# A transformer block in compensated float32: new order of the on-chip memories, MLP weight loads at the value steps, and the first values projected in two steps

## The chip, the cores and the metric

The kernel runs on one core of one Trainium2 chip. Its time is device microseconds (us) of that core, the median of several executions. Before the change it is 1606.38 us, the median of 3 executions (1605.19 to 1607.81).

## What is computed

The input is 16 sequences of 256 tokens with 256 features, 4096 tokens in all. Everything is float32.

```python
x = L0_attn_x                                   # (16, 256, 256)
x = x + layernorm(attn(layernorm(x)))           # 16 heads of 128, causal softmax, W_Q/K/V/O with biases
x = x + layernorm(ffn(layernorm(x)))            # MLP of 2048, gelu(gate) * up, then down
# attn: q, k, v = x @ W_Q, W_K, W_V + biases; scores = q k^T / sqrt(128); softmax; z = attn v; out = z W_O + b_O
# ffn weights: 4-bit codes from a table of 16 values, times one scale for each block of 32
```

## The kernel before

**Arithmetic.** Each float32 operand of a matmul is kept as a rounded high part and a remainder, in two memories whose names end in hi and lo. A product is three matmuls: hi times hi, hi times lo, lo times hi (the helper `three`, L691 to L694). ScalarE (ACT) writes the high part of a fresh PSUM result, VectorE (DVE) the low part by subtraction; for the probabilities and the weights GpSimd (POOL) makes the low part.

**Attention.** The tokens are worked in 8 chunks of 512 (2 sequences). A chunk has 16 steps, one for each head, so there are 128 steps, and n is the step's number, c = n // 16 its chunk and j = n % 16 its place in the chunk. `step_plan(n)` (L97) lists what a step holds, and all engines follow the list in order, each doing its own part. In step n TensorE projects queries and keys of head n+1 (`q`, `k`: 12 matmuls of 512 columns), adds head n-3 to the output projection (`out`), makes `z` of head n-2 and the scores of head n+1. `T` is the turning of the probabilities of head n: VectorE transposes 32x32 blocks of them into `turned`, SyncE's queue (SP) sends that to HBM (`send`, 384 KB) and fetches it back in four pieces (`fetch`, into `back`), which completes the transpose. `pT` is the copy of `back` into high and low parts for `z`. Once in four steps (n % 4 == 1) the values of four heads are projected, four token tiles with 6 matmuls each (`("v", t)`); tiles 0 and 2 are split into high and low parts (`v_hi`, `v_lo`), tiles 1 and 3 are copied whole (`v_late`) for float32 matmuls. The step n = 0 holds the values of the first four heads, all four tiles.

**PSUM.** Three banks (`fbank`) take turns for q, k, v, z and the turned input. A matmul group may start in a bank only when the result three places earlier was read: `bank_free` (L696) waits for VectorE's low part, or for ScalarE's copy of a `v_late` tile.

**Weights of attention.** They are loaded in pairs (256 KB) into `w_raw`, which has room for two pairs. ScalarE copies a pair into its high part (`weights_hi`, L611), GpSimd subtracts to get the low part (`weights_lo`, L1204), and only then may SyncE load the pair after next (L441). Two pairs a step are handled from step 0 on. The projection of head m's queries waits for its pair's low part (L758).

**SyncE.** One queue issues all DMAs in program order: in each step `send`, the pair loads, `fetch`, then whatever else the step has. `fetch` waits until `send` has landed.

**MLP weights.** In chunks 1 to 6 the engines expand the 4-bit MLP weights piece by piece and store them to HBM. After the last use of an attention weight in the last chunk (c = 7), its place in SBUF is filled with MLP weights: 24 units of two loads of 256 KB (`load_w4`, L426). Three units belong to two MLP columns of 128, of which there are 16; TensorE waits for all three before the first gate product of the two (L724). The MLP then runs over 8 chunks, from SBUF alone.

```python
        if c == NCH - 1 and j >= 2:
            load_w4(j - 2)
    for unit in range(HEADS - 2, PIECES // 2):
        load_w4(unit)
```

In chunks 1 to 7 SyncE also stores the block of x after attention of the chunk before in two halves, in steps j = 11 and 13 (`store_x1`). VectorE may write the next chunk's normalised input into the same memory (`stream`, L908) only after both have landed (L937).

Of the kernel before, what the change touches and what calls it, by code (L numbers as in the profile page):

```python
# [4 lines left out]
F32 = mybir.dt.float32  # L5
# [6 lines left out]
P = 128  # L12
# [84 lines left out]
def step_plan(n):  # L97
# [12 lines left out]
    if n == 0:  # L110
        return [("q", 1), ("k", 1), ("scores", 0), *values, ("T", 0), ("scores", 1)]
# [10 lines left out]
    return plan + values if n > 1 and n % HG == 1 else plan  # L122
# [78 lines left out]
class Memory:  # L201

    def __init__(self, nc, ctx):
        def sb(name, shape, dt=F32):
# [4 lines left out]
        self.mask = sb("mask", [P, SEQ])  # L209


        big = sb("weights", [P, 2, PIECES * 2 * P], F32R)
        qk_size = HEADS * 2 * KT * E
        self.wqk_p = [big[:, s, 0:qk_size].rearrange("p (h m k e) -> p h m k e", m=2, k=KT, e=E)
                      for s in range(2)]
        self.wv_p = [big[:, s, qk_size:].rearrange("p (h k e) -> p h k e", k=KT, e=E)
                     for s in range(2)]
        self.w4_all = [big[:, s, :].rearrange("p (n r e) -> p n r e", r=2, e=P) for s in range(2)]
        self.wo_p = [sb(f"wo_{s}", [P, HEADS, D], F32R) for s in ("hi", "lo")]
        self.raw = sb("w_raw", [P, RAW, 2, D])  # L220
# [6 lines left out]
        self.x_res = sb("x_res", [P, TT, D])  # L227
        self.stream = sb("stream", [P, TT, D])
        self.xnT = [sb(f"xnT_{s}", [P, KT, CHUNK], F32R) for s in ("hi", "lo")]
# [49 lines left out]
        self.hbank = [self.ubank[(2 * STEPS_ALL - UB + i) % UB] for i in range(3)]  # L279

# [135 lines left out]
def load_program(sp, mem, s, x_v, w_pairs, biases, words_v, scales_v, w4_v, x1_v, turned_v, out_v):  # L416
# [9 lines left out]
    def load_w4(unit):  # L426
# [8 lines left out]
        for part in range(2):  # L435
            sp.dma_start(mem.w4_all[part][:, at:at + 2].bitcast(F32),
                         w4_v[part][:, 2 * unit:2 * unit + 2]).then_inc(s.w4_all[q], 16)
# [70 lines left out]
    for n in range(STEPS_ALL):  # L508
# [22 lines left out]
        if c == NCH - 1 and j >= 2:  # L531
            load_w4(j - 2)
    for unit in range(HEADS - 2, PIECES // 2):
        load_w4(unit)
# [9 lines left out]
    for c in range(NCH):  # L544
        if c == NCH - 2:
            sp.wait_ge(s.y_stored, 16)
        if c < NCH - 1:

            if c:
                sp.wait_ge(s.xT, c * KT)  # L550
            else:
                sp.wait_ge(s.xn, NCH)
            sp.dma_start(mem.x_in[:], chunk(x1_v, c + 1)).then_inc(s.x, 16)
        if c == NCH - 1:
# [134 lines left out]
def tensor_program(nc, pe, mem, s):  # L689
# [31 lines left out]
    def gate_up(n):  # L721
# [3 lines left out]
        for up, banks in ((0, mem.gbank), (1, mem.hbank)):  # L725
            for kt in range(KT):
                piece = w4_place(3 * (i // 2) + i % 2) + up
                last = three(banks[slot(n)][:], [p[:, piece, kt, :] for p in mem.w4_all],
# [93 lines left out]
    for c, j, kind, m in MLP_STEPS:  # L822
# [16 lines left out]
        else:  # L839
# [6 lines left out]
            for t in range(TT):  # L846
# [3 lines left out]
                             [p[:, k:k + 2, m % 2, :] for p in mem.w4_all],  # L850
# [487 lines left out]
```

## Time and profile before

| | before |
|---|---|
| median of 3 executions | 1606.38 us (1605.19 to 1607.81) |
| profiled execution, its own time | 1606.72 us |
| its span in the trace | 1604.8 us |
| TensorE busy | 1577.9 us, 98% of the span |
| VectorE / ScalarE / GpSimd busy | 66% / 61% / 44% |
| mean granted TensorE clock | 0.998 |

The span is what the trace covers; the own time adds the launch around it (1.9 us). TensorE's busy share says how little it stands still in all (27 us), and its waits by releaser say where. The granted clock is the share of full speed that TensorE had in a stretch: 1.00 is 2.4 GHz, 0.5 is 1.2 GHz.

### The profile page before, as it was taken

The page shows a single profiled execution, that of the slowest core. Times are in us where ns is not written, and L with a number is a line of the kernel's source. Part 1 is how long each engine was busy: PE and PEld are TensorE (multiplying, and loading weights), DVE is VectorE, ACT ScalarE, POOL GpSimd, SP SyncE. Part 2 cuts the span into 40 slices and gives each one's busy share as a digit, 9 for nine tenths or more (in the row PEclk, how much of TensorE's full clock was granted, in tenths as well). Part 3 has the DMA queues.
Part 4 walks back from the last instruction along what each step waited for, and adds up shares of the span by engine and source line. Part 5 has one row for each costly group of instructions (what it writes and reads, how often), then busy time and mean ns, then how long its engine had stood idle before and what let it go on. Part 6 is the DMA issues. An engine that isn't in the chain of part 4 may idle for free.

```text
span 1604.8 us, 28430 instructions
## 1 busy us (share of the span) xinstructions
PE 1577.9 (98%) x9600; PEld 1398.1 (87%) x9600; DVE 1060.9 (66%) x3074; ACT 975.6 (61%) x2433; POOL 711.6 (44%) x1069
## 2 busy tenths in 40 slices
PE   6999999999999999999999999999999999999998
PEld 5888899889888988888889888888888888888887
DVE  4666677677767677677767766665656556565665
ACT  5887677767776777677767766644444444444443
POOL 5764455445554455455445533333333333333333
PEclk9999999999999999999999999999999999999999
DMA  4653434434443444443444455561000010000000
GB/s 122 186 172 116 129 128 149 142 116 142 149 139 119 142 142 137 127 151 126 142 128 136 142 157 162 155 214 40 27 14 27 14 40 27 14 28 14 27 15 25
DMA packets 157440, 167.69 MB, mean 104 GB/s; under 512 B 15856, under 2 KB 130672, under 8 KB 157296
## 3 DMA queue, kind: packets, MB, share of 16 engines
q1 hardware_dynamic: 157296, 165.89, 32.8%
q8 instruction: 76, 1.25, 0.3%
q14 instruction: 68, 0.56, 0.1%
HBM read 94.53 MB, written 71.30 MB: 103 GB/s over the span
## 4 chain that ended last, share of the span: by engine, by line
PE 85%; DMA 6%; ACT 3%; DVE 2%; SPq 2%; issue 1%; POOL 1%; DVEq 0%; POOLq 0%
PE fbank L692 14%; PE fbank L694 14%; PE fbank L693 14%; PE obank L694 7%; PE obank L693 7%; PE obank L692 7%; PE ubank L692 5%; PE ubank L693 5%; PE ubank L694 5%; PE ubank L716 3%; DMA turned_scratch<-turned 3%; PE fbank L794 3%; DMA back<-turned_scratch 2%; SPq L494 2%; ACT probs L589 1%
## 5 line engine op out<-in xcount | busy, mean ns | idle before, releaser
L692 PE MATMUL fbank<-xnT_hi,weights 128*128 128x512 f32 x768 | 305.8, 398 | 1.1 <-DVE xnT_lo L870 1.1
L693 PE MATMUL fbank<-xnT_lo,weights 128*128 128x512 f32 x768 | 304.7, 397 | 0.0
L694 PE MATMUL fbank<-xnT_hi,weights 128*128 128x512 f32 x768 | 304.6, 397 | 0.0
L1238 POOL TENSOR_TENSOR pT_lo<-back,pT_hi 128x512 fp32r<-128x512 f32 x128 | 165.9, 1296 | 284.9 <-ACT pT_hi L654 284.9
L600 ACT ACTIVATE w_raw<-fbank 128x512 f32<-128x512 f32 x128 | 76.4, 597 | 262.7 <-PE fbank L694 262.7
L1200 POOL TENSOR_SCALAR probs<-probs,rsum 128x128 f32<-128x128 f32 (+1 forms) x512 | 208.9, 427 | 20.6 <-DVE rsum L893 16.7
L694 PEld LDWEIGHTS fbank<-xnT_hi,weights 128*128 128x128 f32 x768 | 145.1, 189 | 35.2
L885 DVE CUSTOM_DVE_ANT_0 probs<-ubank,mask 128x128 f32<-128x128 f32 (+1 forms) x512 | 155.0, 355 | 29.1 <-PE ubank L694 28.3
L692 PEld LDWEIGHTS fbank<-xnT_hi,weights 128*128 128x128 f32 x768 | 145.2, 189 | 27.0 <-DVE xnT_lo L870 1.5
L693 PEld LDWEIGHTS fbank<-xnT_lo,weights 128*128 128x128 f32 x768 | 145.2, 189 | 24.7
L974 DVE SCALAR_TENSOR_TENSOR w_raw<-w_raw,fbank 128x512 f32<-128x512 f32 x128 | 87.9, 687 | 113.3 <-ACT w_raw L600 113.3
L1218 POOL TENSOR_TENSOR kT_lo<-probs,kT_hi 128x512 fp32r<-128x512 f32 x64 | 82.8, 1293 | 165.6 <-ACT kT_hi L609 165.6
L980 DVE SCALAR_TENSOR_TENSOR probs<-w_raw,fbank 128x512 f32<-128x512 f32 x128 | 88.0, 687 | 97.9 <-ACT w_raw L604 97.9
L570 ACT ACTIVATE zT_hi<-fbank,bias_v 128x512 fp32r<-128x512 f32 x128 | 87.5, 684 | 106.6 <-PE fbank L794 106.3
L1218 POOL TENSOR_TENSOR v_lo<-probs,v_hi 128x512 fp32r<-128x512 f32 x64 | 82.7, 1292 | 156.4 <-ACT v_hi L609 156.4
L692 PE MATMUL obank<-wo_hi,zT_hi 128*128 128x256 f32 x512 | 143.6, 280 | 0.0
L694 PE MATMUL obank<-wo_hi,zT_lo 128*128 128x256 f32 x512 | 143.4, 280 | 0.0
L693 PE MATMUL obank<-wo_lo,zT_hi 128*128 128x256 f32 x512 | 142.8, 279 | 0.0
L872 DVE SCALAR_TENSOR_TENSOR kT_lo<-fbank,bias_k,kT_hi 128x512 fp32r<-128x512 f32 x128 | 95.8, 749 | 58.9 <-ACT k_early L581 58.6
L1043 DVE STREAM_TRANSPOSE turned<-probs 128x384 f32<-128x384 f32 x256 | 131.5, 552 | 0.7 <-DMA turned_scratch<-turned 0.7
L589 ACT ACTIVATE probs<-probs,nmax 128x256 f32<-128x256 f32 x256 | 126.7, 495 | 0.0
L587 ACT ACTIVATE probs<-probs,nmax 128x128 f32<-128x128 f32 x256 | 100.7, 394 | 15.3 <-DVE nmax L885 11.6
(122 smaller groups left out, 4571.9 us busy)
## 6 DMA issues: line engine op xcount, KB each, us to landing
turned_scratch<-turned SPq DMA_DIRECT2D x128, 384.0 KB, 2.6
back<-turned_scratch SPq DMA_DIRECT2D x512, 96.0 KB, 2.2
w_raw<-in_w_pairs SPq DMA_DIRECT2D x32, 256.0 KB, 3.3
w_hi_scratch<-w_hi SPq DMA_DIRECT2D x48, 128.0 KB, 2.0
w_lo_scratch<-w SPq DMA_DIRECT2D x48, 128.0 KB, 2.0
weights<-w_hi_scratch SPq DMA_DIRECT2D x24, 256.0 KB, 3.6
weights<-w_lo_scratch SPq DMA_DIRECT2D x24, 256.0 KB, 4.1
x_res<-in_x SPq DMA_DIRECT2D x16, 256.0 KB, 2.9
```

The lines of the kernel that those rows point to most:

```text
L587: act.activation(pr[:, 0:P], pr[:, 0:P], ACT.Exp, bias=nmax[:, 0:1], scale=-1.0, accum_out=sums[:, 0:1])
L589: act.activation(pr[:, P:384], pr[:, P:384], ACT.Exp, bias=nmax[:, 1:2], scale=-1.0, accum_out=sums[:, 1:2]).then_inc(s.exp, 1)
L692: nc.tensor.matmul(out, a[0], b[0], start=start, stop=False, skip_group_check=skip)
L693: nc.tensor.matmul(out, a[0], b[1], start=False, stop=False, skip_group_check=skip)
L694: return nc.tensor.matmul(out, a[1], b[0], start=False, stop=stop, skip_group_check=skip)
L872: ins = dve.scalar_tensor_tensor(dst, bank, bias, hi.bitcast(F32), ALU.add, ALU.subtract)
L885: last = dve.tensor_tensor_reduce(out=pr[:, lo:hi], in0=bank[:, lo:hi], in1=mask, scale=-SCALE, scalar=3.0e38, op0=ALU.add, op1=ALU.min, a ...
L980: after(dve.scalar_tensor_tensor(act_v, mem.th[j % 2], 1.0, mem.gbank[slot(n)][:], ALU.add, ALU.mult))
L1043: dve.transpose(mem.turned[:, :, :, b, :].rearrange("p k u j -> p u k j"), mem.probs[b].rearrange("p (u k j) -> p u k j", u=3, k=4)).then_ ...
L1200: last = pool.tensor_scalar(pr[:, lo:hi], pr[:, lo:hi], mem.rsum[i][:, at:at + 1], 1.0, ALU.mult, ALU.mult)
L1218: pool.tensor_tensor(lo, mem.act_v[j % 2], hi.bitcast(F32), ALU.subtract).then_inc(s.iT_lo, 1)
L1238: pool.tensor_tensor(lo[:].rearrange("p u b (a j) -> p (u b) a j", j=32), mem.back[m % 2][:, :, 0:2].rearrange("p a u b j -> p (u b) a j") ...
```

## The change

It has three parts.

1. The order of the SBUF memories. `stream`, `x_res` and `xnT` move from behind the weights to the front, `mask` moves behind the weights, and the one memory `weights`, which held the query/key and the value weights of both parts, becomes four (`wqk_hi`, `wqk_lo`, `wv_hi`, `wv_lo`). A helper `w4_at` finds an MLP piece in them. Sizes and operands are the same.
2. In the last chunk SyncE loads MLP weights only in the steps in which values are projected (j = 1, 5, 9, 13), two units each; 6 more follow behind the last attention step, and the last 10 behind the first load of x of the MLP stage.
3. The first values are projected in two steps: tiles 0 and 1 in step 0, tiles 2 and 3 in step 1, behind the projections of head 2.

```diff
@@ step_plan
     if n == 0:
-        return [("q", 1), ("k", 1), ("scores", 0), *values, ("T", 0), ("scores", 1)]
+        return [("q", 1), ("k", 1), ("scores", 0), *values[:2], ("T", 0), ("scores", 1)]
+    if n == 1:
+        return [("q", 2), ("k", 2), *values[2:], ("T", 1), ("pT", 0), ("scores", 2)]
@@
-    return plan + values if n > 1 and n % HG == 1 else plan
+    return plan + values if n % HG == 1 else plan
@@ Memory
-        self.mask = sb("mask", [P, SEQ])
+        self.stream = sb("stream", [P, TT, D])
+        self.x_res = sb("x_res", [P, TT, D])
+        self.xnT = [sb(f"xnT_{s}", [P, KT, CHUNK], F32R) for s in ("hi", "lo")]
-        big = sb("weights", [P, 2, PIECES * 2 * P], F32R)
...
+        self.wqk_p = [sb(f"wqk_{s}", [P, HEADS, 2, KT, E], F32R) for s in ("hi", "lo")]
+        self.wv_p = [sb(f"wv_{s}", [P, HEADS, KT, E], F32R) for s in ("hi", "lo")]
         self.wo_p = [sb(f"wo_{s}", [P, HEADS, D], F32R) for s in ("hi", "lo")]
+        self.mask = sb("mask", [P, SEQ])
@@
+    def w4_at(self, part, piece):
+        if piece < 2 * HEADS:
+            return self.wqk_p[part][:].rearrange("p h m k e -> p (h m) k e")[:, piece:]
+        return self.wv_p[part][:, piece - 2 * HEADS:]
@@ load_program, in a step
-        if c == NCH - 1 and j >= 2:
-            load_w4(j - 2)
-    for unit in range(HEADS - 2, PIECES // 2):
+        if c == NCH - 1 and j % HG == 1:
+            for unit in (j // 2, j // 2 + 1):
+                load_w4(unit)
+    for unit in range(HEADS // 2, HEADS - 2):
         load_w4(unit)
@@ load_program, MLP
             sp.dma_start(mem.x_in[:], chunk(x1_v, c + 1)).then_inc(s.x, 16)
+        if c == 0:
+            for unit in range(HEADS - 2, PIECES // 2):
+                load_w4(unit)
```

Where SyncE's instructions stand shows part 2. Before, in steps j = 11 and 12 of the last chunk (`back` is the fetch, `x_scratch` the store of x, `weights` the MLP loads):

```order
L484 DMA turned_scratch<-turned 128x768
L494 DMA back<-turned_scratch 32x4x192 x4
L458 DMA x_scratch<-stream 128x2x256
L436 DMA weights<-w_hi_scratch 128x512
L436 DMA weights<-w_lo_scratch 128x512
L484 DMA turned_scratch<-turned 128x768
L494 DMA back<-turned_scratch 32x4x192 x4
L436 DMA weights<-w_hi_scratch 128x512
L436 DMA weights<-w_lo_scratch 128x512
L484 DMA turned_scratch<-turned 128x768
```

The same steps of the changed kernel, and step 13 behind them, up to its first MLP loads:

```order
L488 DMA turned_scratch<-turned 128x768
L498 DMA back<-turned_scratch 32x4x192 x4
L462 DMA x_scratch<-stream 128x2x256
L488 DMA turned_scratch<-turned 128x768
L498 DMA back<-turned_scratch 32x4x192 x4
L488 DMA turned_scratch<-turned 128x768
L498 DMA back<-turned_scratch 32x4x192 x4
L462 DMA x_scratch<-stream 128x2x256
L440 DMA wqk_hi<-w_hi_scratch 128x512
L440 DMA wqk_lo<-w_lo_scratch 128x512
```

Between the send of step 11 and that of step 12 there were two MLP loads, and between those of steps 12 and 13 two more; both pairs are gone.

ScalarE's instructions of step 1 show part 3. Before, from the projections of head 2 to the copy of the probabilities of head 0:

```order
L570 ACTIVATE qT_hi<-fbank,bias_q 128x256
L575 ACTIVATE q_early<-fbank,bias_q 128x256
L570 ACTIVATE kT_hi<-fbank,bias_k 128x512
L581 ACTIVATE k_early<-fbank,bias_k 128x256
L613 ACTIVATE wo_hi<-w_raw 128x512
L613 ACTIVATE weights<-w_raw 128x512
L654 ACTIVATE pT_hi<-back 128x512
```

In the changed kernel:

```order
L578 ACTIVATE qT_hi<-fbank,bias_q 128x256
L583 ACTIVATE q_early<-fbank,bias_q 128x256
L578 ACTIVATE kT_hi<-fbank,bias_k 128x512
L589 ACTIVATE k_early<-fbank,bias_k 128x256
L621 ACTIVATE wo_hi<-w_raw 128x512
L621 ACTIVATE wqk_hi<-w_raw 128x512
L577 ACTIVATE v_hi<-fbank 128x512
L577 ACTIVATE v_late<-fbank 128x512
L662 ACTIVATE pT_hi<-back 128x512
```

The copies of value tiles 2 and 3 now stand behind the two weight copies (`wo_hi` and `wqk_hi`) and ahead of `pT_hi`. On VectorE the low part of tile 2 stands before the transpose of head 1 where nothing stood between that and the low part of the keys. Before:

```order
L872 SCALAR_TENSOR_TENSOR qT_lo<-fbank,bias_q,qT_hi 128x256
L872 SCALAR_TENSOR_TENSOR kT_lo<-fbank,bias_k,kT_hi 128x512
L1043 STREAM_TRANSPOSE turned<-probs 128x3x4x32 x2
L885 ISA probs,nmax<-ubank,mask 128x128
L885 ISA nmax 128x1
```

After:

```order
L880 SCALAR_TENSOR_TENSOR qT_lo<-fbank,bias_q,qT_hi 128x256
L880 SCALAR_TENSOR_TENSOR kT_lo<-fbank,bias_k,kT_hi 128x512
L878 TENSOR_TENSOR v_lo<-fbank,v_hi 128x512
L1051 STREAM_TRANSPOSE turned<-probs 128x3x4x32 x2
L893 ISA probs,nmax<-ubank,mask 128x128
```

So the transpose and the masking of head 2's scores (the ISA rows) come behind `v_lo`, which needs ScalarE's `v_hi`.

## Rows read from the trace of the kernel before

**Rows 1.** The page: busy time of each engine

```profile
PE 1577.9 (98%) x9600; PEld 1398.1 (87%) x9600; DVE 1060.9 (66%) x3074; ACT 975.6 (61%) x2433; POOL 711.6 (44%) x1069
```

**Rows 2.** Waits of TensorE: us in total, times, longest us

```profile
PE fbank L692 <- DVE v_lo L870: 5.5, 5, 3.5
PE ubank L716 <- DVE kT_lo L872: 3.8, 6, 1.9
...
PE fbank L711 <- DVE stream L908: 0.9, 2, 0.6
```

**Rows 3.** Windows of the last chunk: length, busy times, clock, DMA share, GB/s

```profile
1027.50:1031.20 3.70, 0.24 (x2) 0.04 (x1) 1.02 (x3) 3.68 (x12) 2.88 (x5) 1.00 0.61 221
1031.20:1035.60 4.40, 4.40 (x12) 3.49 (x13) 1.49 (x4) 0.74 (x2) 0.01 (x1) 0.61 0.78 208
```

**Rows 4.** Timeline, steps 12 and 13 of the last chunk: start us, us

```profile
1015.44 0.43 SPq L458 DMA_DIRECT2D x_scratch<-stream  x1
1015.97 0.41 SPq L436 DMA_DIRECT2D weights<-w_hi_scratch  x1
...
1016.98 0.38 SPq L484 DMA_DIRECT2D turned_scratch<-turned  x1
1022.78 2.93 SPq L494 DMA_DIRECT2D back<-turned_scratch  x4
...
1027.52 0.63 ACT L654 ACTIVATE pT_hi<-back 128x512 fp32r<-128x512 f32 x1 [4.45 <-DMA back<-turned_scratch]
...
1031.16 0.50 PE L692 MATMUL fbank<-weights,xnT_hi 128*128 128x512 f32 x1 [3.46 <-DVE v_lo L870]
```

**Rows 5.** Timeline of SyncE, step 12 of the chunk before

```profile
887.61 0.41 SPq L484 DMA_DIRECT2D turned_scratch<-turned  x1
890.53 1.74 SPq L494 DMA_DIRECT2D back<-turned_scratch  x4
```

**Rows 6.** Timeline, second store of x, last chunk

```profile
1032.42 0.43 SPq L458 DMA_DIRECT2D x_scratch<-stream  x1
...
1034.80 1.38 DVE L908 TENSOR_SCALAR stream<-x_in,mv,rstd 128x256 f32<-128x256 f32 x4 [2.73 <-DMA x_scratch<-stream]
```

**Rows 7.** Timeline of steps 0 and 1

```profile
19.32 0.40 PE L692 MATMUL fbank<-weights,xnT_hi 128*128 128x512 f32 x1
...
24.62 2.53 POOL L1207 TENSOR_TENSOR weights<-w_raw,weights 128x512 fp32r<-128x512 f32 x2
...
25.01 0.69 DVE L870 TENSOR_TENSOR v_lo<-fbank,v_hi 128x512 fp32r<-128x512 f32 x1 [0.27 <-ACT v_hi L569]
...
27.05 0.95 SPq L442 DMA_DIRECT2D w_raw<-in_w_pairs  x2
...
32.20 1.03 DVE L1043 STREAM_TRANSPOSE turned<-probs 128x384 f32<-128x384 f32 x2
32.34 0.49 PE L716 MATMUL ubank<-k_early,q_early 128*128 128x128 f32 x2 [1.93 <-DVE kT_lo L872]
...
32.65 0.63 ACT L613 ACTIVATE wo_hi<-w_raw 128x512 fp32r<-128x512 f32 x1 [1.15 <-DMA w_raw<-in_w_pairs]
...
34.37 0.63 ACT L654 ACTIVATE pT_hi<-back 128x512 fp32r<-128x512 f32 x1 [0.40 <-DMA back<-turned_scratch]
```

**Rows 8.** DMA issues: form, count, KB each, median us from issue to landing

```profile
w_raw<-in_w_pairs SPq DMA_DIRECT2D x32, 256.0 KB, 3.3
...
weights<-w_hi_scratch SPq DMA_DIRECT2D x24, 256.0 KB, 3.6
```

**Rows 9.** Timeline of TensorE, first and ninth matmul of MLP column 4

```profile
1062.01 0.40 PE L692 MATMUL fbank<-xnT_hi,weights 128*128 128x512 f32 x1
...
1063.88 0.39 PE L694 MATMUL ubank<-xnT_hi,weights 128*128 128x512 f32 x1
```

**Rows 10.** Groups of TensorE with 256 columns: count, busy us, mean ns, idle

```profile
L693 PE MATMUL obank<-wo_lo,zT_hi 128*128 128x256 f32 x512 | 142.8, 279 | 0.0
...
L693 PE MATMUL ubank<-kT_lo,qT_hi 128*128 128x256 f32 x256 | 71.9, 281 | 0.0
```

More of the change, by code:

```diff
@@ L208, in __init__ @@
         self.power = sb("power", [P, TT])
-        self.mask = sb("mask", [P, SEQ])
-        big = sb("weights", [P, 2, PIECES * 2 * P], F32R)
[L213 to L219, printed above, removed]
+        self.stream = sb("stream", [P, TT, D])
[3 more added lines that the diff above has]
+        self.wv_p = [sb(f"wv_{s}", [P, HEADS, KT, E], F32R) for s in ("hi", "lo")]
+        self.wo_p = [sb(f"wo_{s}", [P, HEADS, D], F32R) for s in ("hi", "lo")]
+        self.mask = sb("mask", [P, SEQ])
         self.raw = sb("w_raw", [P, RAW, 2, D])
@@ L226, in __init__ @@
         self.x_in = sb("x_in", [P, TT, D])
-        self.x_res = sb("x_res", [P, TT, D])
-        self.stream = sb("stream", [P, TT, D])
-        self.xnT = [sb(f"xnT_{s}", [P, KT, CHUNK], F32R) for s in ("hi", "lo")]
         self.qT = [[sb(f"qT{i}_{s}", [P, 2, P], F32R) for s in ("hi", "lo")] for i in range(2)]
@@ L435, in load_w4 @@
         for part in range(2):
-            sp.dma_start(mem.w4_all[part][:, at:at + 2].bitcast(F32),
+            sp.dma_start(mem.w4_at(part, at)[:, 0:2].bitcast(F32),
                          w4_v[part][:, 2 * unit:2 * unit + 2]).then_inc(s.w4_all[q], 16)
@@ L727, in gate_up @@
                 piece = w4_place(3 * (i // 2) + i % 2) + up
-                last = three(banks[slot(n)][:], [p[:, piece, kt, :] for p in mem.w4_all],
+                last = three(banks[slot(n)][:], [mem.w4_at(p, piece)[:, 0, kt, :] for p in range(2)],
                              [p[:, kt, :] for p in mem.xnT], kt == 0, kt == KT - 1)
@@ L849, in tensor_program @@
                 last = three(out, [p[:, t * P:(t + 1) * P] for p in mem.iT[m % 4]],
-                             [p[:, k:k + 2, m % 2, :] for p in mem.w4_all],
+                             [mem.w4_at(p, k)[:, 0:2, m % 2, :] for p in range(2)],
                              m == 0 and t % 2 == 0, m == NT - 1, skip=True)
```

## The prediction

> **What bounds the kernel now.** I read the page first. TensorE is busy 1577.9 of 1604.8 us and no other engine over 1061 [rows 1], so only its 27 us of standing still, and stretches in which it runs slowly, can be won. The change adds and removes no matmul. The waits of TensorE by releaser come next. The two large entries that the edits can touch are the wait for `v_lo`, 5.5 us in five waits of which one is 3.5, and the wait for `kT_lo`, 3.8 us in six of which one is 1.9 [rows 2]. The timeline places them: the 3.5 is at 1031.16, in step 13 of the last chunk, ahead of value tile 3 [rows 4]; the 1.9 is at 32.34, ahead of the scores of head 2, in step 1 [rows 7]. Windows around the first show what comes with it: TensorE does nothing from about 1027.5 to 1031.2, and in the 4.40 us behind that its granted clock is 0.61 on the mean, most of it the lower level of 1.2 GHz [rows 3].
>
> **MLP loads at the value steps.** Follow the wait at 1031.16 back. TensorE waits for a PSUM bank that VectorE's `v_lo` frees; that waits for `v_hi` on ScalarE, which works in order, behind `pT_hi` and the exponentials; and `pT_hi` began at 1027.52, after 4.45 us of idleness, on the landing of `back` [rows 4]. The fetch for it was issued at 1022.78, the moment the send of 1016.98 had landed, 5.8 us after its issue. Ahead of that send in the queue are the store of x (1015.44) and one unit of MLP loads, the first at 1015.97 [rows 4]. One chunk earlier the same send has the same store ahead (it stands in the same step) and no such unit, and lands after 890.53 - 887.61 = 2.9 us [rows 5]. So 2.9 us of the lateness belong to the unit that the change removes here. The next unit, between fetch and next send, goes too.
>
> What remains of the wait? `pT_hi` would start 2.9 us earlier, at about 1024.6. The exponentials, `v_hi` and `v_lo` behind it took from 1027.52 to 1031.16; shifted they end at 1028.3, against a need at 1027.7 (1031.16 - 3.46). That leaves 0.6 us. But the issue of the fetch took 2.93 us there against 1.74 one chunk earlier [rows 4, 5], at a place in time that the shifted fetch would have passed by then, which is worth 1.2 us more; so I take 0 as left, with 0.6 as the other end. Without a long wait the slow stretch goes too: 4.40 us at 0.61 lose 4.40 x 0.39 = 1.7 us [rows 3]. Gain: 3.46 + 1.7 = 5.2 us.
>
> Where the stall goes: TensorE now asks for the next chunk's normalised input 5.2 us earlier. VectorE writes it only when the second half of x is stored; before, the store was issued at 1032.42 and VectorE began at 1034.80 [rows 6]. The store stands behind the fetch of step 13, whose send gets 3 to 4 us earlier (it no longer waits for the late fetch and the unit), not 5.2, so it becomes the next to be late. In the other chunks this very wait occurs twice, 0.9 us in all, 0.6 at most [rows 2]. I take 0.4 us, with 0 and 1.5 as ends. In the new value steps four loads (1 MB) go out behind the fetch; a value step is longest before the next send, and one load lands in 3.6 us [rows 8], so these I cost at nothing. If that cover failed, a send would be late as at 1016.98, again some 3 us.
>
> The ends of the loads: 6 units are issued behind the last attention step instead of 10, and the last 10 behind one load of x. MLP column 4 starts at 1062.01 [rows 9] and needs units 6 to 8; unit 8 is now the first of the burst, issued where unit 14 is now, about 10 us ahead of that, and needs 3.6 us [rows 8]. Each later pair of columns has more slack than it loses. I cost this at nothing.
>
> **First values in two steps.** TensorE has the same work ahead of the scores of head 2 in either order: tiles 2 and 3 only change places with the scores of head 1 and the projections of head 2. In the new order the queries of head 2 come at about 23.3 (the values begin at 19.32 [rows 7], two tiles take 12 x 0.234 = 2.8 us by [rows 9], the eight shorter matmuls of head 1's scores some 1.2) and wait for the low part of their weights, the first of the two GpSimd instructions that begin at 24.62 and take 2.53, so until 25.9 [rows 7]. Behind it stand 24 matmuls; the ninth starts 1.87 us behind the first [rows 9], so 0.234 each, 5.6 us, and the scores of head 2 come at 31.5 instead of 32.34: 0.8 us earlier [rows 7], the wait of 1.93 filled by matmuls.
>
> Against this stands what now lies in the way of head 1's transpose. It must wait for `v_lo` of tile 2, that for `v_hi`, and that for two weight copies; the first of these starts at 32.65, when a load issued at 27.05 has landed, 5.6 us later [rows 7]. The median of such a load is 3.3 us [rows 8]. In step 0 the transpose of head 0 loses a `v_lo` ahead of it (0.69 us at 25.01), so the send and the load behind it leave about 0.8 us earlier. Case A, the load is as slow as before: first copy at 31.8, second done at 33.1, `v_hi` and `v_lo` 1.3 us behind, so the transpose begins at 34.3 instead of 32.20 [rows 7], and the steps behind it, which in this phase are a chain from masking to exponentials to the next queries, come 1.2 to 1.8 us later. TensorE stood still 1.9 us at 32.34, has no slack to absorb it, and the whole kernel ends that much later. Case B, the load takes its median: it lands at 29.5, the copies end by 31.4, the transpose begins at 32.7, 0.5 late, while ScalarE, which before was held by `pT_hi` until 35.00 [rows 7] and now gets `back` earlier with the send of head 0, starts its exponentials about as early as before: -0.4 to 0.3 us. The landing is what decides, and both kinds stand in the trace; I take B, as only one load of the first steps was that slow, and 0.0 us. The gain is nothing: the filled wait of 1.93 is given back, because what bounds these steps is the chain, not TensorE.
>
> **Memory order.** Same sizes, same access patterns. The rows that could show a dependence on place are the 256-column matmuls: moving `wo` from one end of SBUF takes 279 ns, moving `kT` from the other 281 [rows 10]. I cost it at nothing. The 512-column matmuls follow each other every 0.234 us [rows 9]. The Trainium skill, TensorE: Matmul & The Clock Gate, gives 215.7 ns start to start for a warm back-to-back matmul of 512 columns, measured on other operands. If the present placement were what costs the difference, and the new one cured it, some 3840 matmuls would save 18 ns each, an estimate from that page of 70 us; by the rows here it saves 0, and the sum goes by the rows.
>
> **Sum.** -5.2 + 0.4 + 0.0 = -4.8 us against the profiled execution's 1606.72, whose own time stands 0.34 above the median. Median after: 1606.38 - 4.8 = 1601.6 us.
>
> **Rivals.**
> - Case A in step 1: the late weight load holds up `v_hi`. For it: 5.6 us for that load [rows 7]. Against: the median of 3.3 [rows 8]. Sum -4.8 + 1.5 = -3.3: 1603.1 us.
> - The clock falls in the first steps. The wait for the weights of head 2 is 25.9 - 23.3 = 2.6 us, between 1.93, after which TensorE kept its clock [rows 7], and 3.46, after which it fell [rows 4, 3]. If it falls, the 12 projections of head 2 take twice as long, 2.8 us more, straight on the chain; with the late copies some 3.5 us in all. Sum -1.3: 1605.1 us.
> - The wait at 1031.16 has another cause, and only part of it goes. For it: the fetch's issue took 2.93 us in that place. If 2.9 us go and the slow clock stays, the gain is about 2.5: 1604 us.
> - Slower than before: the burst. Unit 8 moves from step 10 to behind the last step, among 6 units and x. Column 4 starts at 1062.01 and TensorE waits for whatever is later than that; once the unit lands 5 us later than this, the gain is spent, and at 9 us late the kernel takes 1611 us. Against it: even the tenth load of the present burst is issued before 1062.
> - A dependence on placement, either sign, 1590 us or below, or 1620 us.
>
> **Chances.** Forecast 0.46; case A 0.25; clock in the first steps 0.12; part of the stall stays 0.08; burst 0.06; placement 0.03. A change of 0.2% is 3.2 us, about what a measurement of this kernel can tell from none. The forecast is faster; of case A, which lies at the bound, a bit over half; of placement half: 0.46 + 0.15 + 0.02 = 0.63 faster. Same: 0.10 + 0.12 + 0.08 = 0.30. Slower: 0.07. The likeliest case alone spans 1600.3 (-5.2 - 0.4, and 0.5 for the runs) to 1602.9 (0.6 left of the wait, 0.7 more on the store). The whole range reaches to the clock's case: 1600.0 to 1605.2.
>
> **What would show it.** In the profile after: no wait over 0.6 us for `v_lo` in the last chunk and clock 1.00 there; the send of step 12 landing in about 3 us; a wait of TensorE for a weight's low part near 23.3 to 25.9; the wait at the scores of head 2 gone, and the scores of heads 3 and 4 within 0.5 us of their time before. I am wrong if these last come over 1 us later, if the clock is below 1.00 between 24 and 40, or if the first gate products of the MLP wait for a DMA.

## Result and profile after

The changed kernel takes 1589.97 us, the median of 4 runs (1584.19 to 1591.08), against 1605.85 us before (1605.19 to 1607.81, 4 runs): ratio 0.9892, 95% interval 0.9866 to 0.9918. It is faster, as forecast, but by 16 us where 4.8 were forecast, and the time lies far below the range. The profiled execution has a span of 1588.4 us, 16.4 less than before, and its own time is 1591.08.

The page of the changed kernel, busy times:

```profile
PE 1561.3 (98%) x9600; PEld 1397.9 (88%) x9600; DVE 1061.5 (67%) x3074; ACT 974.1 (61%) x2433; POOL 712.5 (45%) x1069
```

This line already says where the time came from. TensorE has the same 9600 matmuls, and they take 16.6 us less than in [rows 1], while its idle time is the same 27 us. The standstill of 3.5 us that went has made way for others of the same sum. The waits of TensorE (us in total, times, longest us):

```profile
PE ubank L745 <- DVE stream L1008: 5.8, 1, 5.8
PE ubank L724 <- DVE kT_lo L880: 4.4, 8, 1.4
PE fbank L700 <- POOL wqk_lo L1215: 2.7, 1, 2.7
PE fbank L719 <- DVE stream L916: 2.4, 4, 1.0
PE fbank L700 <- DVE v_lo L878: 1.8, 4, 0.6
```

The wait of 3.5 us for `v_lo` of [rows 2] is gone. A new one of 2.7 us, for the low part of a weight, has come; the waits for the normalised input are four instead of two.

**Three places tell how the 16.4 us are spread.** First, the scores of the last two heads of attention, in the changed kernel and then in the one before (start us, us):

```profile
1019.92 0.39 PE L724 MATMUL ubank<-k_early,q_early 128*128 128x128 f32 x2
...
1033.06 0.39 PE L724 MATMUL ubank<-k_early,q_early 128*128 128x128 f32 x2
```

```profile
1022.19 0.44 PE L716 MATMUL ubank<-k_early,q_early 128*128 128x128 f32 x2
...
1040.54 0.39 PE L716 MATMUL ubank<-k_early,q_early 128*128 128x128 f32 x2
```

Up to the first of them 2.3 us are won (1022.19 - 1019.92), and between them 5.2: this stretch took 18.35 us and takes 13.14. It is step 13 with the stall. The other 8.9 us of the 16.4 are won behind it, in the MLP. There, the matmuls that turn x stand once in each chunk. The view of one tile gives their first and last start between 1100 and 1330 us, before and after:

```profile
L711 PE MATMUL fbank<-ident,x_in x16: 270/281/288, 1114.0 to 1319.4; 128*128 128x128 f32 x16
```

```profile
L719 PE MATMUL fbank<-ident,x_in x16: 270/283/283, 1105.4 to 1307.5; 128*128 128x128 f32 x16
```

Three chunks took 205.4 us and take 202.1, so 1.1 us less each, 8.8 over 8 chunks. Nothing in these chunks was changed but where the memories stand. The matmuls themselves show it. MLP column 4 of the changed kernel, its first and its ninth matmul:

```profile
1061.23 0.40 PE L700 MATMUL fbank<-xnT_hi,wqk_hi 128*128 128x512 f32 x1
...
1063.05 0.39 PE L702 MATMUL ubank<-xnT_hi,wqk_lo 128*128 128x512 f32 x1
```

Eight steps take 1.82 us where they took 1.87 [rows 9]: 227.5 ns a matmul, not 234. I shall use the six matmuls of one projection of queries or keys as the measure, start of the first to start of the next group, the median over the kernel: 1.40 us before, 1.36 after. With 256 columns nothing moved (118 ns a matmul before and after).

**The stall** is gone as forecast. The same two windows as [rows 3], with busy times of TensorE, its weight loads, VectorE, ScalarE and GpSimd, then the granted clock:

```profile
1027.50:1031.20 3.70, 3.66 (x24) 3.03 (x23) 2.44 (x6) 2.38 (x5) 0.00 (x0) 1.00 0.81 266
1031.20:1035.60 4.40, 4.40 (x34) 4.15 (x33) 3.99 (x14) 2.88 (x8) 1.04 (x1) 1.00 0.23 91
```

And SyncE's timeline of steps 12 to 14, where the dots stand for the four loads behind the store of x:

```profile
1013.99 0.34 SPq L488 DMA_DIRECT2D turned_scratch<-turned  x1
1016.37 1.74 SPq L498 DMA_DIRECT2D back<-turned_scratch  x4
1020.36 0.34 SPq L488 DMA_DIRECT2D turned_scratch<-turned  x1
1023.45 1.74 SPq L498 DMA_DIRECT2D back<-turned_scratch  x4
1025.23 0.43 SPq L462 DMA_DIRECT2D x_scratch<-stream  x1
...
1032.26 0.32 SPq L488 DMA_DIRECT2D turned_scratch<-turned  x1
1034.62 1.74 SPq L498 DMA_DIRECT2D back<-turned_scratch  x4
```

The send of step 12 lets the fetch go 2.4 us after its issue, where it took 5.8 [rows 4], and the issue of the fetch is back at 1.74.

**The first steps** are not as forecast. TensorE at the queries of head 2, and windows around it:

```profile
25.90 0.77 PE L700 MATMUL fbank<-xnT_hi,wqk_hi 128*128 128x512 f32 x1 [2.69 <-POOL wqk_lo L1215]
...
26.47 0.63 PE L701 MATMUL fbank<-xnT_lo,wqk_hi 128*128 128x512 f32 x1
...
26.90 0.63 PE L702 MATMUL fbank<-xnT_hi,wqk_lo 128*128 128x512 f32 x1
```

```profile
22.93:25.90 2.97, 0.28 (x3) 0.10 (x2) 2.14 (x7) 1.44 (x4) 2.93 (x6) 0.95 0.00 0
25.90:29.30 3.40, 3.40 (x9) 2.69 (x10) 1.08 (x8) 2.33 (x10) 2.74 (x5) 0.54 0.82 258
```

After standing still from 23.2 to 25.90, TensorE ran for some 3 us at a granted clock near 0.5, that is 1.2 GHz, and its matmuls follow each other every 430 ns. Head 2's scores come at 32.93, 0.6 later than in [rows 7], where 0.8 earlier was forecast.

### The profile page after: what moved, and what is told of

Read it like the earlier page. It is cut to its first block, busy times and chain, and to the rows that moved or that the text cites. A ratio compares the mean times of both kernels' runs of the same rounds, so it can differ in the third digit from the quotient of the medians.

```text
span 1588.4 us, 28430 instructions
## 1 busy us (share of the span) xinstructions
PE 1561.3 (98%) x9600; PEld 1397.9 (88%) x9600; DVE 1061.5 (67%) x3074; ACT 974.1 (61%) x2433; POOL 712.5 (45%) x1069
## 4 chain that ended last, share of the span: by engine, by line
PE 79%; DMA 6%; ACT 6%; DVE 5%; SPq 3%; issue 1%; POOL 1%; DVEq 0%; POOLq 0%
PE fbank L700 13%; PE fbank L701 13%; PE fbank L702 13%; PE obank L702 6%; PE obank L701 6%; PE obank L700 6%; PE ubank L700 5%; PE ubank L702 5%; PE ubank L701 5%; DMA turned_scratch<-turned 3%; PE ubank L724 3%; PE fbank L802 2%; DMA back<-turned_scratch 2%; SPq L498 2%; ACT probs L597 1%
## 5 line engine op out<-in xcount | busy, mean ns | idle before, releaser
L700 PE MATMUL fbank<-xnT_hi,wqk_hi 128*128 128x512 f32 x768 | 302.9, 394 | 3.7 <-POOL wqk_lo L1215 2.7
L701 PE MATMUL fbank<-xnT_lo,wqk_hi 128*128 128x512 f32 x768 | 301.3, 392 | 0.0
L702 PE MATMUL fbank<-xnT_hi,wqk_lo 128*128 128x512 f32 x768 | 300.7, 392 | 0.0
L702 PEld LDWEIGHTS fbank<-xnT_hi,wqk_lo 128*128 128x128 f32 x768 | 145.1, 189 | 31.8
L700 PEld LDWEIGHTS fbank<-xnT_hi,wqk_hi 128*128 128x128 f32 x768 | 145.2, 189 | 27.6 <-issue 2.9
L701 PEld LDWEIGHTS fbank<-xnT_lo,wqk_hi 128*128 128x128 f32 x768 | 145.3, 189 | 22.5
```

The costliest lines, as they stand in the source:

```text
L700: nc.tensor.matmul(out, a[0], b[0], start=start, stop=False, skip_group_check=skip)
L701: nc.tensor.matmul(out, a[0], b[1], start=False, stop=False, skip_group_check=skip)
L702: return nc.tensor.matmul(out, a[1], b[0], start=False, stop=stop, skip_group_check=skip)
```

## Experiments

All times are medians. The ratio is that of the means, to the kernel before on the same chip, with its 95% interval, so it can differ a little from the ratio of the medians. Where memories stand follows from their order and sizes, each rounded up to 32 bytes, one behind the other. I give the place of `xnT` and of the weights as bytes from the start of the partition, modulo 512. Before, `xnT` stands at 352 and the weights at 160: between them lie multiples of 512 and three bias memories of 64 bytes. In the changed kernel both stand at 160.

### The three parts apart

The edits are the parts of the diff: the order of memories alone, the loads alone, the first values alone, and the first two together.

> Only the order of the memories is changed. Theory 1 (the placement of the operands sets how fast 512-column matmuls follow each other): the six-matmul groups take 1.36 us as in the changed kernel instead of 1.40, the MLP stage is 8 to 9 us shorter, attention is at most 3 us shorter because it is bound by the chain of scores, exponentials and projections, and the whole is 9 to 12 us below before, near 1596. Rival (the gain comes from the MLP loads and the values, and the faster matmuls go with some other effect of them): the time stays within 2 us of before and the groups stay at 1.40 us.

> Only the MLP loads are moved. The wait of 3.46 us for v_lo in step 13 of the last chunk is gone and with it the slow clock behind it: 4 to 5.5 us below before, near 1601, with groups of six matmuls at 1.40 us as before. Rival (the stall was not caused by the loads): under 1.5 us gained.

> Only the first values are projected in two steps. Theory (the wait for head 2's weights lets the clock fall, and the late v_lo holds up head 1's transpose): 0.5 to 2.5 us above before, with a wait of 2.7 us for a weight's low part near 23 and a clock below 1.00 between 25.9 and 29. Rival (it is the filled wait that counts): 0.5 to 1.5 us below before.

> The changed kernel without the values in two steps. If the three parts add up, it is 0.5 to 2.5 us below the changed kernel and about 14 to 17 us below before. Rival (the values in two steps help): it is above the changed kernel.

| part | us | ratio |
|---|---|---|
| memories alone | 1590.47 | 0.9918 (0.9904 to 0.9933) |
| loads alone | 1598.38 | 0.9968 (0.9955 to 0.9980) |
| first values alone | 1604.99 | 1.0005 (0.9994 to 1.0015) |
| memories and loads | 1587.30 | 0.9899 (0.9884 to 0.9915) |

Before was 1603.49 here. The memories, which I had costed at nothing, bring 13 us. The loads bring 5.1. The first values can't be told from nothing: the interval reaches from 1.0 us gained to 2.4 lost. The first two together have the lowest median of this study, though their ratio can't be told from the changed kernel's 0.9892. In the loads' kernel the slow clock is gone as well: TensorE's clock is 1.00 in all of 1015 to 1035. In the kernel with the first values alone the clock falls in the same place as above, and stays low for twice as long:

```profile
22.93:25.90 2.97, 0.17 (x3) 0.04 (x1) 2.16 (x7) 1.42 (x4) 2.94 (x6) 0.87 0.00 0
25.90:29.30 3.40, 3.40 (x8) 2.72 (x9) 1.06 (x8) 2.34 (x10) 2.75 (x5) 0.50 0.76 254
...
25.20:31.90 6.70, 6.01 (x14) 4.78 (x15) 2.25 (x12) 3.21 (x11) 3.45 (x6) 0.50 0.67 198
```

Its scores of head 2 come at 34.29, 2.0 us later than in [rows 7], and yet those of the last head at 1040.63, 0.1 later than before. In this pair of traces the loss of the first steps is made good on the way. It is one pair, and executions of one kernel differ by more than 2 us, so a loss of that size at the end isn't excluded.

### Which property of the place

Four kernels. The first is the kernel before with one bias memory moved, so that `x_in` to `xnT` start 64 bytes lower. The second is the new order with two bias memories moved to the front: `xnT` 64 bytes higher, the weights 128. The third is the kernel before with only `stream`, `x_res` and `xnT` moved ahead of the weights. The fourth has the four weight memories of the change, and `xnT` where it was.

```diff
 kernel before, first experiment
-        self.bias_q = sb("bias_q", [P, HEADS])
         self.bias_k = sb("bias_k", [P, HEADS])
...
         self.xnT = [sb(f"xnT_{s}", [P, KT, CHUNK], F32R) for s in ("hi", "lo")]
+        self.bias_q = sb("bias_q", [P, HEADS])
```

> Before, with x_in, x_res, stream and xnT 64 bytes lower in each partition and all else in place, so that xnT starts at 32 instead of 96 beyond a multiple of 128 bytes. Theory A (this offset of the moving operand sets the pace): groups of six matmuls at 1.36 us, time about 9 to 12 us below before. Theory B (the distance of xnT from the weights, or the end of SBUF in which it lies, sets it): groups stay at 1.40 us and the time within 2 us of before.

> The new order of the memories alone, with stream, x_res and xnT 64 bytes higher and the weights 128 bytes higher, so that xnT starts at 96 beyond a multiple of 128 bytes as it did before, and the weights at 32 as ever. Theory A: groups of six back at 1.40 us, time near before. Theory B: groups at 1.36 us, time near that of the new order, about 1590.

> Before, with stream, x_res and xnT moved to the front and the weights left as the one memory. It has xnT at 32 beyond a multiple of 128 and near the front: both theories give 1.36 us for six matmuls. A third theory, C (splitting the weights in four does it, or their order), gives 1.40 us.

> The weights as four memories as in the changed kernel, and stream, x_res and xnT where they were before (xnT at 96). Theories A and B both give 1.40 us for six matmuls and no gain; theory C gives 1.36 us and 9 to 12 us gained.

| xnT / weights | order | six matmuls of q or k | us | ratio |
|---|---|---|---|---|
| 288 / 160 | before | 1.40 us | 1605.26 | 0.9993 (0.9978 to 1.0009) |
| 224 / 288 | new | 1.395 | 1596.94 | 0.9945 (0.9920 to 0.9969) |
| 160 / 160 | x in front | 1.36 | 1593.64 | 0.9911 (0.9882 to 0.9940) |
| 352 / 160 | before, weights in four | 1.40 | 1605.46 | 0.9995 (0.9983 to 1.0007) |

Two of the three theories fall: A, the offset modulo 128 (the first experiment has the good one, and its groups are slow), and C, the split. Of B the place at the front falls too (the second kernel's groups are there and slow). Its other half, the distance of `xnT` from the weights, is left, and in a sharper form: in the kernels with quick groups the two operands of one matmul start at the same offset. The second kernel gains for another reason: its 256-column matmuls take 114 to 115 ns instead of 118. They are 3072, in the output and the down projections, which makes 9 to 10 us.

### Equal offsets, or one good offset

The first is the kernel before with all three small biases moved behind `xnT`, so that it stays far back but at 160. In the next two the new order gets one bias memory at the very front (224 and 224), or between `xnT` and the weights (160 and 224). In the last, small memories are arranged so that all large ones start at multiples of 512.

> The kernel before, with only the three small q, k and v bias memories (64 bytes a partition each) moved from ahead of x_in, x_res, stream and xnT to behind them, so that these start 192 bytes lower; xnT stays where it was otherwise, far behind the other memories, and the weights stay. The normalized input xnT then starts at 160 modulo 512 bytes, where the weights (the other operand of the same matmuls) also start at 160; before it was 352 against 160. Theory R (a 512-column matmul is at its quick pace when both of its operands start at the same offset modulo 512 bytes, or a divisor of it): six-matmul groups of 1.36 us in place of 1.40, an MLP chunk 1.1 us shorter, and the time 9 to 13 us below before, as when x stood at the front (0.9911). Theory Abs (it is xnT's own offset, 160 modulo 512): the same. Rival N (xnT must stand near the start of the memory, whatever its offset, beside not being shifted by 64): groups stay at 1.40, time within 2 us of before.

> The new order of memories alone (no change of loads or first values), with one 64-byte bias memory put ahead of everything, so that both xnT and the weights start 64 bytes higher: 224 and 224 modulo 512. Theory R (equal offsets): groups stay at 1.36 us and the time at that of the new order alone (0.992 of before). Theory Abs (xnT's own offset of 160): groups of 1.39 to 1.40, time within 0.4 per cent of 0.996 to 1.000.

> The new order alone, with one 64-byte bias memory put between x and the weights: xnT stays at 160 modulo 512 bytes, the weights and what stands behind them start 64 bytes higher, at 224. Theory R (equal offsets): the pace is lost, groups of 1.38 to 1.40 us, time 0.996 to 1.000 of before. Theory Abs (xnT's own offset): groups stay at 1.36, time 0.992.

> The new order and the new loads (the changed kernel without its third part, 0.9899 of before), with the small memories arranged so that every large one, xnT, weights, qT, kT, v, zT and the probabilities, starts at a multiple of 512 bytes. Theory R (equal offsets): groups of 1.36 us or a little less, 0.988 to 0.990 of before; if the score, value and projection matmuls also run by the offsets of their operands, up to 3 us less than that. Theory Abs (160 is the good offset): groups of 1.40, 0.996 of before (the loads alone).

| xnT / weights | six of q or k | MLP gate / up | us | ratio |
|---|---|---|---|---|
| 160 / 160, far back | 1.36 us | 1.37 / 1.36 | 1591.71 | 0.9924 (0.9909 to 0.9939) |
| 224 / 224 | 1.37 | 1.39 / 1.38 | 1604.64 | 1.0002 (0.9992 to 1.0012) |
| 160 / 224 | 1.40 | 1.40 / 1.40 | 1609.63 | 1.0034 (1.0022 to 1.0047) |
| 0 / 0, with the loads | 1.36 | 1.39 / 1.36 | 1591.43 | 0.9921 (0.9906 to 0.9936) |

The first row is the cleanest: moving 192 bytes of biases brings 0.76%. The third loses the gain by 64 bytes. So it is not `xnT`'s own offset, and unequal offsets of these two were slow in every case. But equal ones aren't all: at 224 and 224 the groups are in between, and its output projection is slower too, 284 ns a matmul against 279 in [rows 10] (the length of one, of which the next begins before the end):

```profile
L695 PE MATMUL obank<-wo_lo,zT_hi 128*128 128x256 f32 x512 | 145.3, 284 | 0.0
```

That kernel is no faster than before. Its time is the one that theory Abs gave (0.996 to 1.000), but its groups of 1.37 in attention are not. The edit did more than it was meant to: it also brought the weights 64 bytes closer to the other operand of the 256-column matmuls (`zT`, and the memories of `kT` and `v` that hold the MLP's product), and these follow each other every 120.4 ns instead of 117.7. On 3072 matmuls that takes 8 us back. In the fourth kernel they take 119.4 ns, and it is no faster than new order and loads without the shifts (0.9899).

### The matmuls by themselves

The group of six without the rest of the kernel. The memories hold constants, and nothing of the block is computed:

```python
for kt in range(2):
    ws = [fixed[:, w + s * W_LO + kt * P:w + s * W_LO + (kt + 1) * P] for s in range(2)]
    xs = [moving[:, x + s * X_LO + kt * 512:x + s * X_LO + kt * 512 + cols] for s in range(2)]
    for a, b in ((0, 0), (0, 1), (1, 0)):
        last = nc.tensor.matmul(bank[:, 0:cols], ws[a], xs[b], start=n == 0, stop=n == 5)
        n += 1
```

> The disputed cost by itself. This kernel computes nothing of the reference (its output is a copy of x). TensorE alone runs the six-matmul group of the projections on memories of constants, without a wait: hi and lo of the moving operand 4096 bytes apart, of the stationary one 32768, 512 columns, high and low in the kernel's order. Part 1: for each of 16 differences d between the start of the stationary and of the moving operand (0, 32, ... 480 modulo 512 bytes), each of 16 places of the moving one (0, 32, ... 480), two groups; 3072 matmuls in order of d. Part 2: each d again with the moving operand at 160 and 352, 8 groups each, while VectorE copies 512 columns in SBUF without a pause. Part 3: each d with 256 columns. Theory R (the difference of the offsets decides, and TensorE's own two reads are what collides): in part 1 matmuls follow each other every 227 ns at d = 0 and every 230 to 236 at the differences of the slow kernels (d = 320 as in before, 384, 64), and the same for all places of one d. Rival S (the slow pace needs the other engines' traffic on SBUF; only the presence of VectorE's copies matters): part 1 has the same pace, 227 or less, at every d, and part 2 is slower at some. Rival V (the values or the waits of the real kernel matter, not place): one pace in all three parts.

Windows of 43.6 us from the first part, in which TensorE works alone; (x) is how many matmuls start in one. The differences are 32, 64, 96, 128, 160, 192, 224 and 256 bytes:

```profile
80.20:123.80 43.60, 43.60 (x190) 1.00 0.00 1
124.80:168.40 43.60, 43.60 (x189) 1.00 0.00 0
169.50:213.10 43.60, 43.60 (x188) 1.00 0.00 1
214.40:258.00 43.60, 43.60 (x189) 1.00 0.00 0
259.10:302.70 43.60, 43.60 (x188) 1.00 0.00 1
303.90:347.50 43.60, 43.60 (x192) 1.00 0.00 0
347.90:391.50 43.60, 43.60 (x189) 1.00 0.00 1
392.70:436.30 43.60, 43.60 (x192) 1.00 0.00 0
```

The clock is 1.00 and TensorE never pauses, yet two of the eight stretches hold more matmuls. From start to start, over the 192 matmuls of each difference (over the second half of the very first, behind the rise of the clock):

| stationary minus moving, bytes | 0 | 32 | 64 | 96 | 128 | 160 | 192 | 224 |
|---|---|---|---|---|---|---|---|---|
| ns, 512 columns | 229.4 | 232.3 | 232.9 | 234.0 | 232.6 | 233.7 | 229.0 | 233.1 |
| the same plus 256 bytes | 229.6 | 232.3 | 232.9 | 234.0 | 232.6 | 233.7 | 229.0 | 233.1 |
| ns, 256 columns | 119.5 | 118.2 | 116.7 | 117.5 | 119.1 | 119.8 | 117.8 | 117.1 |

The place of the moving operand at a given difference changes up to 1.7 ns with 512 columns. With 256 it changes 3 ns at the difference of 64: 118.2 with the moving operand at 0 or 256, 115.2 to 115.5 at 128 or 384. So theory R holds in part. The difference decides, modulo 256 bytes in place of 512, but it need not be 0: 192 is quick too.

The kernel before has, for queries and keys, a difference of 160 - 352, which is 320 modulo 512 or 64 modulo 256: 232.9 ns here, 233 there. After has 0: 229.4 here, 227 there. The 229.4 holds the groups behind each change of place, which are slower. In the second part four groups in a row have one place, and the second to fourth of them follow each other every 226.8 ns at 0 and every 233.3 at 64, as in the kernel. Rival S is out: TensorE alone tells the two differences apart (229.4 and 232.9 ns). With VectorE's copies running at both, 48 matmuls take 10.93 us at 0 and 11.18 at 320 (227.8 and 233.0 ns). Rival V is out as well.

The values are a check that the experiments didn't plan. In their matmuls `xnT` is the stationary operand and the weights the moving one, so the kernel before has a difference of 352 - 160 = 192 there. First and thirteenth matmul of a value step:

```profile
799.65 0.39 PE L692 MATMUL fbank<-weights,xnT_hi 128*128 128x512 f32 x1
...
802.40 0.39 PE L692 MATMUL fbank<-weights,xnT_hi 128*128 128x512 f32 x1
```

That is 229 ns a matmul, in the same kernel in which queries and keys take 233, and 229.0 in the table. Over whole kernels the value groups take 1.38 us at 192, 1.40 at 128 (the kernel with `xnT` at 288) and 1.36 at 0. The Trainium skill, SBUF — State Buffer, section "A bandwidth-pool intuition that's wrong", lists a second, independent read port for the weight loads next to the moving operand's. The trace doesn't bear out that the two reads have nothing to do with each other: with only TensorE at work, the pace follows the difference of their addresses, 229 to 234 ns.

### The map applied

In the first two, seven or eight small memories serve as spacers in the kernel with new order and new loads, so that every pair of operands has the difference that was best alone. The third sets `xnT` and the weights of the new order 256 bytes apart.

```diff
 first experiment; the memories named here were elsewhere
+        self.bias_q = sb("bias_q", [P, HEADS])
+        self.nmax = [[sb(f"nmax{i}{b}", [P, 2]) for b in range(2)] for i in range(2)]
         self.kT = [[sb(f"kT{i}_{s}", [P, CHUNK], F32R) for s in ("hi", "lo")] for i in range(2)]
...
+        self.sums = [sb(f"sums{i}", [P, 4]) for i in range(2)]
+        rsum_first = sb("rsum0", [P, 4])
+        self.stats = sb("stats", [P, TT, 6])
         self.pT = [sb(f"pT_{s}", [P, 2, 2, P], F32R) for s in ("hi", "lo")]
...
+        self.rsum = [rsum_first, sb("rsum1", [P, 4])]
+        self.mv = sb("mv", [P, TT, 2])
         self.zT = [sb(f"zT_{s}", [P, CHUNK], F32R) for s in ("hi", "lo")]
```

> The changed kernel without its third part (1587.3 us), with seven small memories used as spacers so that every matmul's pair of operands stands at the difference (stationary minus moving, modulo 256 bytes) that was quickest when TensorE ran alone: 0 for the 512-column matmuls (xnT and the weights both at 160), 64 for those of 256 columns (zT, kT and v at 224 against the weights at 160, qT at 32 against kT at 224, v at 224 against pT at 160; before this zT, kT and v stood 192 from the weights, and qT and pT 0 from their partners). Theory R (the pairs' differences decide): 512-column groups stay at 1.36 us, the output and down projections fall from 118 to 115 or 116.5 ns a matmul; 1536 of these in the MLP, where TensorE alone sets the pace, give 2.3 to 4.6 us, the rest of attention little: 1583 to 1585. Rival (one pair in the MLP is not all, other engines' access to the shifted memories takes the gain back, as at 224 and 224): 1587 or above.

> As the one before, with one more small memory moved so that all large memories stand 32 bytes lower: weights, xnT and pT at 128 modulo 256, kT, v and zT at 192, qT at 0. The differences are the same; with TensorE alone 256-column matmuls took 115.0 ns here at difference 64, against 117.9 with the moving operand at 0. Theory R: 512-column groups at 1.36 us, output and down projections at 115 ns, 4.6 us below the changed kernel without its third part: about 1583. Rival (as at 224 and 224 and at 0 and 0, a place other than 160 lets the MLP's gate groups slow to 1.39): 16 groups a chunk, 8 chunks, 0.02 us each, 2.2 us back: 1585 to 1587.

> The new order alone, with small memories of 256 bytes in all between xnT and the weights (and 192 more behind the weights): xnT stays at 160, the weights start at 416 modulo 512 bytes, and all other pairs keep their differences modulo 256. If the difference counts modulo 256, as with TensorE alone (227 to 229 ns at 0 and at 256): groups of 1.36 us, 0.992 of before, as the new order has. If it counts modulo 512 in the kernel: groups of 1.38 to 1.40 us, 0.997 or above.

| | six of q or k | MLP gate / up | projections, 256 columns | us | ratio |
|---|---|---|---|---|---|
| all pairs, weights at 160 | 1.36 us | 1.39 / 1.36 | 118 ns | 1588.54 | 0.9895 (0.9879 to 0.9910) |
| all pairs, weights at 128 | 1.36 | 1.39 / 1.36 | 118 | 1589.61 | 0.9898 (0.9881 to 0.9914) |
| 256 bytes apart | 1.36 | 1.37 / 1.36 | 118 | 1594.33 | 0.9933 (0.9919 to 0.9948) |

The third answers its question: the period is 256 bytes in the whole kernel too. The first two missed. The 256-column matmuls stayed at 118 ns and did not fall to 115, and the gate groups slowed from 1.37 to 1.39 though their own operands did not move against each other. So the map for 512 columns carries over, and that for 256 columns in part: 117.7 ns at 192 and 119.4 at 0 in whole kernels are the table's values, but at 64 one kernel has 114.4 (weights at 288) and these two 117.8, and at 128 there are values from 117.9 to 120.4. Neither can be told from the 0.9899 of the new order and loads.

## Why the prediction was wrong

**The step that failed is "Memory order".** It reads "I cost it at nothing". It measured 13.1 us alone (0.9918 of 1603.49), which is the whole miss. I looked for a dependence on place with the wrong pair of rows: the two groups of 256 columns differ in how far apart their operands stand, and both kinds happen to take 118 ns from start to start. The 279 and 281 ns that I compared are the lengths of single matmuls, which overlap, and `wo` stands in the middle of SBUF, not at one end. I treated the place as a property of one memory (which end of SBUF), where it is one of a pair. I compared no row of 512-column matmuls with another, though the trace of before had a hint: its value groups take 1.38 us and its queries and keys 1.40, with the same columns and clock, and the roles of the operands exchanged. A group of queries also alternates between 231 and 236 ns. I gave the rival on placement 0.03 and a time of "1590 us or below", which is where the time fell (1589.97). No sum stood behind that figure, so this is luck.

How 13 us come of it: the 3840 matmuls of 512 columns run some 6 ns quicker, those of the values 3, 21 us in all. The 1536 of the MLP (16 columns, 8 chunks, 12 each) give 9.2 us, and 8.9 arrive, since TensorE hardly waits there. The 2304 of attention (1536 of queries and keys, 768 of values) hold 12 us, of which 2 to 5 arrive: heads there hang on the chain from masking to the next queries, and waits for `kT_lo` and for the input grew (from 0.9 us in two to 2.4 in four). The 70 us that I had estimated from the 215.7 ns of the Trainium skill, TensorE: Matmul & The Clock Gate, were no guide to the size either: the best pace of a group in any run here was 226.5 ns.

**MLP loads: right, but for the small term.** Forecast -5.2 and +0.4. Alone they measured -5.1 (0.9968), and step 13 shrank by 5.2. The send landed in 2.4 us, no wait for `v_lo` there is above 0.6, and the clock is 1.00. In the value step, the send of 1020.36 was 3.1 us from its fetch, before the loads go out, and the next, at 1032.26 after four loads, 2.4. The store of x did become the next to be late, and VectorE waited 1.2 us for it. But TensorE waited for the input in no place of the last chunk, so the 0.4 us for it came to nothing.

**First values: the size right, the way wrong.** I took 0.0 and measured +0.8 (1.0005, interval on both sides of 1). But what I gave 0.12 is what happened: the wait for the low part of head 2's weights was 2.7 us, and the clock fell. The landing of the load, which I had said decides, did not. In the changed kernel ScalarE copied `wo_hi` at 31.34 with no wait for a DMA, right behind the keys (`k_early`) that the slow matmuls had made late, and head 1's transpose began at 33.61 instead of 32.20. With this part alone the loss at the scores of head 2 was 2.0 us, and at heads 3 to 10 1.3 to 2.5. The 3.5 us that I gave this rival at the end did not arrive (the interval ends at 2.4). My claim that TensorE "has no slack to absorb it, and the whole kernel ends that much later" is not borne out by the trace of that part alone, in which 0.1 us was left at the last head, but one pair of traces doesn't settle it.

**What stays open.** Why the gate groups of the MLP run at 1.37 in some placements and at 1.39 in others with the same difference of their own operands; it moves with memories that these matmuls don't read. Another engine's accesses are one candidate. The matmuls just before are another: the gate groups stand behind the down projection, whose operands are 192 bytes apart modulo 256 in every kernel with 1.37 and at another difference in those with equal offsets and 1.39, and with TensorE alone the first group behind a change of place took 1.38 us at a difference of 0, where settled groups take 1.36. Neither was tested in the kernel. The output projection is open in the same way: in the kernels at 224 / 224 and 160 / 224 its own operands stand alike, and it takes 120.4 and 117.9 ns. Nor is it known what a difference does inside the chip, and why the 256-column matmuls gained in one kernel (weights at 288, `zT` at 352) and in no other. The difference of 192, quick for 512 columns in the test and for the values, was tried for queries, keys and the MLP in no kernel.

## What to carry to other kernels

When a change moves memories, compare the byte offsets of the two operands of each frequent matmul, modulo 256, before and after; an order that only inserts 64 bytes between them can cost 1% of a kernel that TensorE bounds (1.0034 against 0.9918 of before, where the 64 bytes moved other pairs too). A shift that helps one pair can hurt another, so list all of them. Look for it in the trace as the start-to-start time of matmuls of one kind within an unbroken group, not in busy shares: an engine at 98% can still be 3% slow. Where the chain bounds a stage, as in attention here, quicker matmuls give back only a part, and a stall of the first steps may cost nothing at the end.

## What the runs showed of the hardware

- The start-to-start time of 512-column matmuls with TensorE alone depends on the difference of the two operands' addresses modulo 256 bytes: 229 ns at 0 and 192, 232 to 234 at the other multiples of 32, at a granted clock of 1.00. At 0 it settles at 226.8 ns once a few groups have the same place.
- 256-column matmuls have another map: 116.7 ns at 64, 119.8 at 160, and 119.5 at 0, where 512 columns are quick.
- The length of a standstill did not decide whether the clock fell. In the changed kernel it was 1.2 GHz for some 3 us behind one of 2.7 us; with the memories alone one of 2.70 us, in step 13 of the last chunk, left it at 1.00. Behind 1.93 us in step 1 it stayed at 1.00 in the kernel before [rows 7], and fell in the one with `xnT` far back at 160. The wait and windows behind it in the kernel with the memories alone, the window behind the wait of [rows 7], and wait and window in the kernel with `xnT` far back:

```profile
1025.77 0.50 PE L694 MATMUL fbank<-wv_hi,xnT_hi 128*128 128x512 f32 x1 [2.70 <-DVE v_lo L872]
...
1025.80:1027.00 1.20, 1.20 (x5) 1.01 (x6) 0.69 (x1) 0.15 (x1) 0.03 (x1) 1.00 0.37 106
1027.00:1030.00 3.00, 3.00 (x14) 2.25 (x12) 0.38 (x2) 1.44 (x3) 0.00 (x0) 1.00 0.90 246
```

```profile
32.34:39.25 6.91, 5.61 (x32) 4.56 (x32) 3.72 (x15) 5.86 (x17) 5.62 (x8) 1.00 0.57 181
```

```profile
31.54 0.49 PE L716 MATMUL ubank<-k_early,q_early 128*128 128x128 f32 x2 [1.93 <-DVE kT_lo L872]
...
32.20:35.60 3.40, 3.40 (x13) 2.92 (x12) 1.66 (x10) 1.69 (x6) 2.79 (x3) 0.50 0.90 266
```
